# Layer 2 attention heads: who turns the 32x32 blocks of the inverse, which banks the query projections use, and the order of three engines' work

## The reference

```python
q = silu(causal_conv(x @ Wq)); k = silu(causal_conv(x @ Wk)) * 128**-0.5; v = silu(causal_conv(x @ Wv))
alpha, beta = sigmoid(x @ Wa + ba), sigmoid(x @ Wb + bb)
for t in range(256):                                   # S is 128 x 128 for each sequence and head
    err = S @ k[t] - v[t]
    S = alpha[t] * S - beta[t] * outer(err, k[t])
    o[t] = S @ q[t]
out = (layernorm(o) * sigmoid(x @ Wg)) @ Wo
```

## Time and profile before

| | us |
|---|---|
| median of 3 runs (2211.37 to 2226.61) | 2215.23 |
| the profiled execution, its own time | 2214.98 |
| its span, first to last instruction | 2213.2 |
| the heads of layer 2, first to last level product | 1052 to 1718 |

### The profile page before, as it was taken

One profiled execution on the slowest core, in us unless ns is written; L12 is line 12 of the kernel. 1 busy time (PEld: TensorE's weight loads), 2 busy tenths in 40 slices (PEclk: granted clock), 3 DMA queues, 4 the chain that ended last, 5 costly groups with the idle time before them and its releaser, 6 DMA issues. The chain is left out here.

```text
span 2213.2 us, 52159 instructions
## 1 busy us (share of the span) xinstructions
PE 1847.7 (83%) x21053; PEld 1275.8 (58%) x21053; DVE 1218.2 (55%) x3265; ACT 879.8 (40%) x2049; POOL 473.0 (21%) x542
## 2 busy tenths in 40 slices
PE   4886789895999896666999999999999797679669
PEld 1345644563777563554766666666676674446446
DVE  6867532344664336645566666676666226642741
ACT  4523311222552222224666677667666203220120
POOL 0022300330000332642212221222121003720200
PEclk7897989996999997887999999999999798789779
DMA  7000000514200516751000010001000317830000
GB/s 266 18 1 1 1 1 16 176 39 156 111 1 19 177 37 215 246 217 51 21 33 22 22 42 22 22 22 42 22 22 22 84 27 218 262 148 18 1 3 19
DMA packets 55331, 157.37 MB, mean 71 GB/s; under 512 B 12899, under 2 KB 29881, under 8 KB 50822
## 3 DMA queue, kind: packets, MB, share of 16 engines
q1 hardware_dynamic: 45206, 128.84, 17.5%
q0 software_dynamic: 9888, 25.20, 3.4%
HBM read 115.36 MB, written 40.48 MB: 70 GB/s over the span
## 5 line engine op out<-in xcount | busy, mean ns | idle before, releaser
L2362 PE MATMUL l_heads_ps_p<-xnT,l2a_w 128*128 128x512 f32 x512 | 266.3, 636 | 20.5 <-ACT l_heads_shaped L2681 8.1
L2768 DVE SCALAR_TENSOR_TENSOR l_heads_taps<-l_heads_padded,l2a_conv,l_heads_taps 128x1024 f32<-128x1024 f32 x144 | 187.9, 1323 | 9.7 <-ACT l_heads_taps L2595 8.9
L2362 PEld LDWEIGHTS l_heads_ps_p<-xnT,l2a_w 128*128 128x128 f32 x512 | 87.4, 194 | 84.3 <-issue 57.9
L198 PE MATMUL norm_turn<-zeros,ident 128*128 128x512 f32 x120 | 65.1, 698 | 52.1 <-PEq L60 52.1
L2941 POOL TENSOR_TENSOR l_heads_e<-l2a_table,l_heads_row 128x512 f32<-128x512 f32 x32 | 33.3, 1042 | 327.1 <-DVE l_heads_first L2779 325.3
L189 ACT ACT_TABLE_LOAD x10 | 12.8, 1283 | 204.1 <-PEq L60 204.1
L2594 ACT COPY l_heads_padded<-l_heads_ps_p 128x512 f32<-128x512 f32 x96 | 57.1, 595 | 53.6 <-PE l_heads_ps_p L2362 53.6
L2595 ACT ACTIVATE l_heads_taps<-l_heads_ps_p,l2a_conv 128x512 f32<-128x512 f32 x96 | 76.7, 799 | 0.0
L198 PEld LDWEIGHTS norm_turn<-zeros,ident 128*128 128x128 f32 x120 | 25.9, 224 | 85.5 <-issue 85.5
L1984 ACT ACTIVATE l_heads_e<-l_heads_logit,l_heads_shift 128x128 f32<-128x128 f32 (+1 forms) x128 | 56.6, 443 | 44.7 <-DVE l_heads_shift L2016 44.6
L2944 POOL TENSOR_SCALAR_AFFINE_SELECT l_heads_e<-l_heads_e 128x512 f32<-128x512 f32 x64 | 67.0, 1047 | 9.8 <-POOL l_heads_e L2941 0.6
(11 more groups left out here) (717 smaller groups left out, 4833.8 us busy)
## 6 DMA issues: line engine op xcount, KB each, us to landing
l_results<-zeros SPq DMA_DIRECT2D x24, 512.0 KB, 5.7
l_ffn_a_w_in<-in_l_in_w SPq DMA_DIRECT2D x8, 1536.0 KB
l_ffn_b_w_in<-in_l_in_w SPq DMA_DIRECT2D x8, 1536.0 KB, 10.5
l2a_w<-in_l_w_heads SPq DMA_DIRECT2D x16, 512.0 KB, 3.9
l_heads_row<-l_rows SPq DMA_DIRECT2D x16, 512.0 KB, 4.6
l_ffn_a_w_out<-in_l_out_w SPq DMA_DIRECT2D x8, 768.0 KB
l_ffn_a_w_in<-l_results SPq DMA_DIRECT2D x8, 768.0 KB, 6.5
l_ffn_b_w_out<-in_l_out_w SPq DMA_DIRECT2D x8, 768.0 KB, 8.3
```

The lines of the kernel that those rows point to most:

```text
L198: pe.matmul(turn[:, i % KC, (i // KC) % HALVES, :], core.ident[:], core.zeros[:, 0:HALF], start=True, stop=True)
L2362: mm = pe.matmul(ps_p[half][:], w[b][:, which, c, :], core.xnT[:, c, half * HALF:(half + 1) * HALF], start=(c == 0), stop=(c == KC - 1))
L2768: dve.scalar_tensor_tensor(out=taps[which][:], in0=padded[which][:, :, j:j + SEQ], scalar=conv[p % 2][:, which, j:j + 1], in1=taps[which][ ...
```

## The change

- The turned blocks are no longer made on PE. DVE turns them 32 x 32 by 32 x 32 (`dve.transpose`): the first ones from M (`turn_first`, four instructions for a chunk), at each level the power straight from bank b00 or b10 into `mt`, and the end result from `mz` to Y (`turn_z`, four instructions for a chunk). PE's second product of each level, its zT and its `turn_first` go, with the ACT copies that took them.
- Level 4 forms both halves (64 columns) like the others; the last product has all four blocks, and DVE adds it to Z.
- The power of chunk 1 at levels 1 to 3 is copied to `mz` by ACT (`keep_power`), and DVE waits for it (`power_kept`) before it turns the same bank; of chunk 0 DVE copies it. ACT copies the blocks for `inner_x` (`keep_z`).
- The query projections go to b01 and b11, which the turned powers leave free (`projected`); p0 and p1 keep k, o, v, g. PE, ACT (`take`) and DVE (`convolve`) use the new names.
- PE: level 1 of the next head moves to the end of a head, around the last `multiply`; `turn_values(1)` goes behind level 4 and `turn_o` half 0 ahead of `last_update`; `turn_values(0)` behind it.
- ACT: `shape_o` half 0 goes ahead of the scaled v of chunk 0, and `take` V half 0 behind `take_x`.
- DVE: the second tap of V moves from the end of a head to behind level 1 of the next.

The core of the diff (left out: the renamed banks in `project_from`, `take`, `convolve`, the new semaphores, the removed `turn_first` of PE, two more waits of the same kind as those shown):

```diff
@@ -2170,15 +2170,17 @@
     order.update({f"b{c}{i}": [] for c in range(2) for i in range(3)})
+    for c in range(2):
+        order[f"b{c}1"] += [("q", 0)]
     for h in range(-1, HEADS2):
...
                 order[f"b{c}0"] += [(f"m{n}", h) for n in range(1, LEVELS2 + 1)] + [("z", h), ("w32", h), ("w64", h)]
-                order[f"b{c}1"] += [(f"mt{n}", h) for n in range(1, LEVELS2 + 1)] + [("zT", h), ("x", h), ("corner", h)]
+                order[f"b{c}1"] += ([("q", p)] if more else []) + [("x", h), ("corner", h)]
                 order[f"b{c}2"] += [("qk", h)] + ([("k_end", h)] if c == 0 else []) + [("v", h)]
         for half in range(2):
-            order[f"p{half}"] += [("k", p), ("q", p)] if more else []
+            order[f"p{half}"] += [("k", p)] if more else []
             order[f"p{half}"] += [("o", h - 1)] if h >= 1 else []
...
@@ -2371,48 +2381,27 @@
                 if n == 1:
-                    pe.wait_ge(read[MT_BANK[c]], nth[MT_BANK[c], "mT", h])
+                    pe.wait_ge(first_turned[c], h + 1)
                 else:
                     pe.wait_ge(read[f"b{c}0"], nth[f"b{c}0", f"m{n - 1}", h])
-                    pe.wait_ge(read[f"b{c}1"], nth[f"b{c}1", f"mt{n - 1}", h])
                 begin(f"b{c}0", f"m{n}", h)
                 for s in S:
-                    if n == 1:
-                        for q in BLOCKS:
-                            mm = pe.matmul(bank[c][0][q, s, 0:2 * BK], mt[c][q, s, :], first_and_eye(c, s, q),
-                                           start=True, stop=True)
-                    elif n < LEVELS:
-                        for q in BLOCKS:
-                            mm = pe.matmul(bank[c][0][q, s, 0:2 * BK], mt[c][q, s, :],
-                                           mz[c][q, s].rearrange("p a n -> p (a n)"), start=True, stop=True)
-                    else:
-                        for q in BLOCKS:
-                            mm = pe.matmul(bank[c][0][q, s, BK:2 * BK], mt[c][q, s, :], mz[c][q, s, 1, :],
-                                           start=True, stop=True)
+                    for q in BLOCKS:
+                        moving = first_and_eye(c, s, q) if n == 1 else mz[c][q, s].rearrange("p a n -> p (a n)")
+                        mm = pe.matmul(bank[c][0][q, s, 0:2 * BK], mt[c][q, s, :], moving, start=True, stop=True)
                 mm.then_inc(filled[f"b{c}0"], 1)
-                begin(f"b{c}1", f"mt{n}", h)
+
+            def last_update(c, h):
+
+                pe.wait_ge(read[f"b{c}0"], nth[f"b{c}0", f"m{LEVELS}", h])
                 for s in S:
                     for q in BLOCKS:
-                        mm = pe.matmul(bank[c][1][q, s, 0:BK], m_first(c, s)[q, q] if n == 1 else mz[c][q, s, 0, :],
-                                       mt[c][q, s, :], start=True, stop=True)
-                mm.then_inc(filled[f"b{c}1"], 1)
-
-            def last_update(c, h):
-
-                pe.wait_ge(read[f"b{c}0"], nth[f"b{c}0", f"m{LEVELS}", h])
-                pe.wait_ge(read[f"b{c}1"], nth[f"b{c}1", f"mt{LEVELS}", h])
-                for s in S:
-                    for q in BLOCKS:
-                        mm = pe.matmul(bank[c][1][q, s, 0:BK], mz[c][q, s, 1, :], mt[c][q, s, :], start=True, stop=True)
-                mm.then_inc(filled[f"b{c}1"], 1)
-                for s in S:
-                    for q in (B0, B1, B2):
                         mm = pe.matmul(bank[c][0][q, s, 0:BK], mt[c][q, s, :], mz[c][q, s, 1, :], start=True, stop=True)
...
-                pe.wait_ge(inner_ready[c], h + 1)
+                pe.wait_ge(diagonal_ready[c], 2 * h + 1)
                 begin(f"b{c}0", "w32", h)
...
@@ -2508,12 +2488,11 @@
                 key_key(c, 0)
-                turn_first(c, 0)
+            level(1, 0, 0)
+            level(1, 1, 0)
...
                 p, more = h + 1, h + 1 < HEADS2
-                level(1, 0, h)
-                level(1, 1, h)
                 query_key(0, h)
@@ -2525,16 +2504,16 @@
                     project(p, K, "k", 1)
-                turn_values(1, h)
                 level(4, 0, h)
...
                     project(p, Q, "q", 0)
-                turn_values(0, h)
+                turn_values(1, h)
+                if h >= 1:
+                    turn_o(h - 1, 0)
                 last_update(0, h)
                 last_update(1, h)
-                if h >= 1:
-                    turn_o(h - 1, 0)
+                turn_values(0, h)
                 if more:
...
@@ -2569,16 +2549,18 @@
                 if more:
-                    turn_first(0, p)
                     project_from(p, G, "g", 1, 0)
                 pe.wait_ge(read["b10"], nth["b10", "ks", h])
+                pe.wait_ge(diagonal_ready[1], 2 * h + 2)
                 pe.wait_ge(read["b11"], nth["b11", "corner", h])
...
                     project_from(p, G, "g", 1, 1)
-                    turn_first(1, p)
+                    level(1, 0, p)
                 pe.wait_ge(read["b11"], nth["b11", "u", h])
                 multiply("b12", "o", h, lambda s: qk[1][:, s, :], lambda s: u[1][:, s, :])
+                if more:
+                    level(1, 1, p)
             turn_o(HEADS2 - 1, 0)
...
@@ -2624,30 +2607,17 @@
-            def take_first(c, p):
-                name = MT_BANK[c]
-                act.wait_ge(filled[name], nth[name, "mT", p])
-                if p >= 1:
-                    act.wait_ge(filled[f"b{c}1"], nth[f"b{c}1", "x", p - 1])
-                act.copy(mt[c][:], tile_of_bank[name][:, :, 0:BK]).then_inc(read[name], 1)
-
-            def take_level(n, c, h):
-                name = f"b{c}1"
-                act.wait_ge(filled[name], nth[name, f"mt{n}", h])
-                act.copy(mt[c][:], bank[c][1][:, :, 0:BK]).then_inc(read[name], 1)
-
-            def take_inverse(c, h):
-
-                name = f"b{c}1"
-                act.wait_ge(filled[name], nth[name, "zT", h])
-                if h >= 1:
-                    act.wait_ge(filled[U_BANK[c]], nth[U_BANK[c], "u", h - 1])
-                for q in (B1, B3):
-                    last = act.copy(Y[c][q, :, q], bank[c][1][q, :, 0:BK])
-                last.then_inc(inner_ready[c], 1)
-                for q in (B2, B0):
-                    last = act.copy(Y[c][q, :, q], bank[c][1][q, :, 0:BK])
-                last.then_inc(read[name], 1)
+            def keep_power(n, h):
+
+                act.wait_ge(filled["b10"], nth["b10", f"m{n}", h])
+                act.copy(mz[1][:, :, 0, :], bank[1][0][:, :, 0:BK]).then_inc(power_kept, 1)
+
+            def keep_z(c, h):
+
+                act.wait_ge(read[f"b{c}0"], nth[f"b{c}0", "z", h])
+                for q, at in ((B0, 0), (B2, 0), (B1, BK)):
+                    last = act.copy(z[c][q, :, at:at + BK], mz[c][q, :, 1, :])
+                last.then_inc(z_ready[c], 1)
@@ -2694,23 +2664,18 @@
             act.wait_ge(affine_ready, 2)
-            for c in range(2):
-                take_first(c, 0)
...
                 p, more = h + 1, h + 1 < HEADS2
-                take_level(1, 0, h)
-                take_level(1, 1, h)
+                keep_power(1, h)
                 if more:
                     exps(p, 0)
-                take_level(2, 0, h)
-                take_level(2, 1, h)
+                keep_power(2, h)
                 if more:
...
                     silu(h, V)
-                take_level(3, 0, h)
-                take_level(3, 1, h)
+                keep_power(3, h)
                 if h >= 1:
@@ -2723,16 +2688,17 @@
                     take(p, Q, "q", 0)
-                scaled("b02", "v", h, bv[0], 0, B)
-                take_inverse(0, h)
-                take_inverse(1, h)
                 if h >= 1:
                     shape_o(h - 1, 0)
+                scaled("b02", "v", h, bv[0], 0, B)
+                keep_z(0, h)
+                keep_z(1, h)
                 if more:
                     take(p, Q, "q", 1)
-                    take(p, V, "v", 0)
                 take_x(0, h)
                 take_x(1, h)
+                if more:
+                    take(p, V, "v", 0)
                 if h >= 1:
@@ -2745,11 +2711,8 @@
                 scaled("b12", "qs", h, o_state, 1, FROM_START)
-                if more:
-                    take_first(0, p)
                 whole("b11", "u", h, u[1])
                 if more:
-                    take_first(1, p)
                     take_gate(p, 1)
...
@@ -2781,16 +2745,25 @@
+            def turn_first(c, p):
+
+                dve.wait_ge(read[KK_BANK[c]], nth[KK_BANK[c], "kk", p])
+                pairs = first_of[c][:, 0:2 * PAIR].rearrange("p (a n) -> p a n", n=PAIR)[:, :, 0:2 * P]
+                each = pairs.rearrange("p a (b n) -> p a b n", n=P)
+                for q in BLOCKS:
+                    last = dve.transpose(mt[c][q].rearrange("p (a b) n -> p a b n", b=2), each[q, :, :, q])
+                last.then_inc(first_turned[c], 1)
+
             eyes = eye.unsqueeze(1).broadcast_to([P, SY, BK])
...
```

(46 more changed lines are left out.)

28 lines of the change are left out of this document (10 added, 18 removed).

## The result

| | median, us | lowest to highest | profiled execution's span |
|---|---|---|---|
| before, beside the changed kernel | 2217.57 | 2211.37 to 2226.61, four runs | 2213.2 |
| after | 2284.21 | 2279.65 to 2289.58, four runs | 2277.9 |

The ratio is 1.030, with an interval of 1.0265 to 1.0333: the change costs 3%, 67 us. The forecast was 2225, with a range that ended at 2262. The time is slower and outside the range.

What follows compares the result with a forecast made beforehand. PE was taken to pace the heads: 41.9 us without gaps plus 2.3 for halved clock is 44.2 against 43.71, over 16 heads +10 us on 2214.98, so 2225; range 2180 to 2262.

Steps and rivals of the forecast that it cites:

- What bounds the kernel, and the gaps: PE paces the heads; its "issue" gaps, waits for instruction blocks, would go with fewer matmuls: -1.85 us a head.
- fourth rival: "Issue" gaps stay besides the new waits, not hanging on the number of instructions: 2244 us, chance 0.15.
- matmul count: PE's matmuls in a head would fall from 942 to 638.
- Chain one: From the last `multiply` to level 4, through ACT's `keep_power(3)`: 11.85 us; PE waits 2.6 us around its level-4 products.
- Chain two: ACT's list up to V half 0, behind `take_x`, delays G half 0: level 4 to G 12.7 us, +0.7.
- From G to the last `multiply`: PE's stretch from G half 0: -0.8 for `turn_first`, +0.5 for level 1, +0.4 waiting for r: +0.1 us.
- Turns on VectorE: Each DVE transpose 0.28 us, adding 3.5 us a head; DVE goes from 29.4 to 33 us, `inner_w(1)` covered.
- third rival: Turns on DVE are dear, so `inner_w(1)` waits for Y and level 4 comes later: 2273 us, chance 0.17.
- The clock: PE's new waits are followed by halved clock, 1.6 us a stretch, 1.4 counted a head: +2.3, bounds 0 and 3.2.
- the clock stays up: First rival: PE's clock isn't halved in the new waits, 41.9 us a head: 2187 us, chance 0.24.
- PE alone decides: Second rival: both chains are shorter than thought, a head loses 1.85 and 5.0 us: 2105 us, chance 0.04.
- wrong if heads still alternate: Named sign against the forecast: heads still taking short and long times in turn, as in the kernel before.

Runs made afterwards that it cites:

- x7_small: x3_both plus 16 useless 32 x 32 products on PE behind each level product, eight times a head: 2201.03 us, 0.994 of the kernel before.
- b1_vlate: The kernel before with one edit, ScalarE taking V half 0 behind `take_x`: 2263.6 us, 1.022 of the kernel before.
- x5_fillboth: The changed kernel with useless projections on PE, two before G half 0 and two between the level-4 products: 2206.8 us, 0.997 of the kernel before.
- x3_both: The changed kernel with V half 0 taken ahead of `take_x` and `keep_power(3)` ahead of the second exponential: 2171.93 us, 0.979 of the kernel before.
- x2_kp3: The changed kernel with only `keep_power(3)` on ScalarE moved ahead of the second exponential: 2217.23 us, a single run.

## Why the prediction was wrong

**What bounds the kernel, and the gaps: right.** The "issue" gaps are gone from the heads, as predicted, x7_small brings them back, and they lie at the ends of instruction blocks, as I had read them. The fourth rival (gaps stay) falls. The matmul count was a slip: twelve products of 32 go (eight turned powers, two zT, two `turn_first`), not ten, so 942 - 384 + 16 = 574, which is what the windows show.

**Chain one: right, a little short.** PE's last level-1 product, directly behind the last `multiply`, starts at 1434.78, and the second level-4 product at 1447.19: 12.4, where I took 11.85. The level-3 copy is where it was forecast (PE first, then ACT):

```profile
1434.78 0.65 PE L2391 MATMUL l_heads_bank<-l_heads_first,l_heads_mt 32*32 32x64 f32 x32
...
1443.21 0.72 ACT L2608 ACTIVATE l_heads_e<-l_heads_e,l_heads_log_scale 128x512 f32<-128x512 f32 x1 [2.04 <-POOL l_heads_e L2930]
...
1446.20 0.25 ACT L2613 COPY l_heads_mz<-l_heads_bank 128x128 f32<-128x128 f32 x1
```

That is 11.4 us after 1434.78 (11.3 predicted). From the copy to the product it is 1.0, where I had 0.75, and the 0.2 that I took off the sum had no row behind it. Waits: 2.8 (2.6 predicted).

**Chain two: right, a little short.** From the second level-4 product to G half 0 it is 13.0 (1447.19 to 1460.19), where I had 12.7; `keep_z` takes 1.83 instead of 1.65, and 0.94 instead of 0.7 is waited before the second `inner_x`. G's wait is 1.68 (1.8 predicted). b1_vlate shows the chain alone.

**From G to the last `multiply`: too short.** In the kernel before this is 17.18 (1165.23 to 1182.41 in the earlier trace rows); I added 0.1. At full clock it is 17.70 (1423.12 to 1440.82 in x5_fillboth; x3_both has 17.71). So a head with the new chains and without clock loss is 12.42 + 13.0 + 17.7 = 43.1, which x5_fillboth measures as 43.12, where I had 41.9. These three terms were 1.2 us a head off, 19 us in all. That alone would have given 2244; with my upper bound for the clock besides, 2259. Both are within the range.

**Turns on VectorE: right.** Two of the three groups of the lines view, by form (the third, M, has 302 ns):

```profile
L2766 DVE STREAM_TRANSPOSE l_heads_mt<-l_heads_bank 128x128 f32<-128x128 f32 x128 | 39.2, 306 | 34.6 <-ACT l_heads_mz L2613 32.7 <-PE l_heads_bank L2391 1.6
L2786 DVE STREAM_TRANSPOSE l_heads_y<-l_heads_mz 32x128 f32<-32x128 f32 x128 | 38.7, 303 | 3.0
```

0.306 and 0.303 us against 0.28, close to the 311 ns of the Trainium skill ("VectorE: DVE Perf Modes", "The three transpose paths"), which it gives for bf16. DVE is busy 33.05 a head (33 predicted). The third rival (turns dear, 2273) came nearest in time and is wrong in its cause: x3_both has the same turns and is about 2% faster than before, and in the changed kernel `inner_w` doesn't wait for Y.

**The clock: this is the step that failed.** I wrote: "Price of a halved stretch: 3.22 - 1.98 = 1.25 on one projection, and 0.35 on what follows: 1.6. I count 1.4 a head: +2.3; bounds are 0 and 2 x 1.6 = 3.2." The price of a short stretch was right: 3.4 us at half clock cost 1.6 in x2_kp3. The assumption beneath was wrong, that a wait is followed by one stretch of that size and the clock then recovers, because it did so behind the gaps of the kernel before, where all five stretches were of 3.3 to 3.4 us. With the waits of both chains in every head, it stayed at half for 13.7 us in five of the 13 heads and for 10.2 in a sixth. Forecast were 1.4 stretches, some 4.5 us at half clock in a head; measured are 10.0 (129.8 / 13). The cost is 47.6 - 43.1 = 4.5 instead of 2.3, close to half of the 10.0. The upper bound of 3.2 wasn't one, since nothing in the trace of before showed what such waits at two places of each head do. 2.2 for the clock and 1.2 for the path, times 16, are 54 us; 2225 + 54 = 2279, and the profiled execution took 2279.65. That the path was too short by 1.2 hid nothing and helped nothing: both errors went the same way.

**The rivals.** That the clock stays up (2187) is false for the changed kernel, but it is what the kernel does once the waits are filled (2206.8) or shortened (2171.93). That PE alone decides (2105) is refuted by its waits of 5.4 us a head.

**Signs I had named.** I wrote "wrong if heads still alternate". They do, 44.6 and 50.9, not for the gaps but for the clock: the sign pointed at the step that failed. The granted clock, for which I had given near 0.93, is 0.90 over the 13 heads.

## What to carry to other kernels

A wait of PE costs its own length only while the clock stays up. When a change adds waits of 1.5 to 2 us at two places of a loop, price the clock for the whole loop and not for one projection, and leave the range open upwards if the trace of before has no such loop. Before giving up an idea that came out slower, look at the granted clock of its windows, then move the one instruction that each wait hangs on; here two moved calls on ScalarE turned +3.0% into -2.1%. Where the chain can't be shortened, useless matmuls in the wait are a quick test of whether the clock is what is lost. The gaps under "issue" can be read in the same way: count PE's instructions from one to the next, and see whether a block of instructions lands shortly before each ends.
